# GpSimd's order inside a slot of the expert loop: the split of the expert's activation ahead of the layer chains' step

## The reference, cut to what matters

```python
x = x + 0.5 * moe(layernorm(x))        # 16 experts, top 4, gated: down((up + 1) * glu)
x = x + ssm(layernorm(x))              # long convolution, gelu(exact), projection, inner layernorm
x = x + 0.5 * moe(layernorm(x))        # the same experts again
x = x + 0.5 * lora_moe(layernorm(x))   # 8 + 2 null experts of rank 16, top 2
x = x + attention(layernorm(x))        # 16 heads of 8
x = x + 0.5 * lora_moe(layernorm(x))
```

## The kernel before

| engine | steps |
|---|---|
| VectorE | stats 0, scan_in 5, scan 6, resid 10, inner_stats 11, b_stats 20 |
| GpSimd | norm 0, y 7, gelu_lo 9, inner_norm 12, add 16, b_norm 21 |
| ScalarE | rows 3, gelu 8, inner_rows 14, b_rows 23 |
| TensorE | t1 0, t2 4, proj 10, inner_t1 11, inner_t2 15 |

## Time and profile before

### The profile page before, as it was taken

How to read it: one execution, slowest core, us unless ns; L and a number is a source line. 1 busy time by engine, 2 the same in 40 slices (tenths; PEclk the granted TensorE clock), 3 DMA queues, 4 the chain that set the end, 5 groups by cost and what they waited for, 6 DMA issues and landing times.

```text
span 752.4 us, 11122 instructions
## 1 busy us (share of the span) xinstructions
PE 665.9 (89%) x3617; PEld 389.8 (52%) x3617; DVE 485.5 (65%) x1264; ACT 544.8 (72%) x762; POOL 272.7 (36%) x298
## 2 busy tenths in 40 slices
PE   3798899889999999999876679999999999999857
PEld 2576677667667687777654532322323333333244
DVE  4888979879898999889756542344323445544343
ACT  4765575677768676755334669999999999999722
POOL 3377476866767665556501610112000000000010
PEclk9999999999999999999958789999999999999955
DMA  9001333222332233333200299000099200000000
GB/s 255 29 1 38 111 108 98 86 96 98 90 98 99 88 117 106 99 113 113 64 20 0 66 194 187 4 1 1 15 187 198 51 1 1 2 1 15 16 2 28
DMA packets 31374, 54.54 MB, mean 72 GB/s; under 512 B 4640, under 2 KB 13312, under 8 KB 29808
## 3 DMA queue, kind: packets, MB, share of 16 engines
q1 hardware_dynamic: 30128, 53.38, 26.9%
q0 software_dynamic: 224, 0.34, 0.2%
q10 hardware_dynamic: 960, 0.07, 0.1%
HBM read 35.72 MB, written 1.28 MB: 49 GB/s over the span
## 4 chain that ended last, share of the span: by engine, by line
PE 36%; ACT 23%; DVE 16%; issue 13%; POOL 10%; DMA 1%; ACTq 1%; DVEq 0%; POOLq 0%
ACT raw_w L951 16%; PE bank L1920 7%; POOL act_parts L686 6%; PE bank L1895 5%; PE bank L1596 5%; PE bank L1598 4%; PE bank L1597 4%; DVE act L1215 3%; DVE bank L1204 2%; DVE up L1193 2%; DVE stats L1052 2%; POOL rstd L633 2%; PE bank L1732 1%; ACT xt L777 1%; PE bank L1729 1%
## 5 line engine op out<-in xcount | busy, mean ns | idle before, releaser
L951 ACT ACTIVATE raw_w<-bank,minus_c 128x1024 f32<-128x1024 f32 x256 | 260.8, 1147 | 5.6 <-PE bank L1920 4.5
L686 POOL TENSOR_TENSOR act_parts<-act,act_parts 128x512 fp32r<-128x512 f32 x128 | 168.0, 1316 | 92.8 <-ACT act_parts L850 89.1
L850 ACT ACTIVATE act_parts<-act 128x512 fp32r<-128x512 f32 x128 | 80.8, 632 | 99.9 <-DVE act L1215 99.7
L1440 DVE TENSOR_TENSOR bank<-bank,fix 128x256 f32<-128x256 f32 x128 | 55.3, 433 | 150.8 <-PE bank L1895 150.8
L1596 PE MATMUL bank<-xn_parts,w_hi 128*128 128x512 f32 x256 | 108.3, 423 | 10.2 <-DVE up L1193 6.2
L1193 DVE TENSOR_SCALAR up<-bank,b_up 128x512 f32<-128x512 f32 x128 | 95.3, 744 | 24.4 <-PE bank L1598 21.4
L1598 PE MATMUL bank<-xn_parts,w_hi 128*128 128x512 f32 x256 | 101.4, 396 | 0.0
L1597 PE MATMUL bank<-xn_parts,w_lo 128*128 128x512 f32 x256 | 101.1, 395 | 0.0
L630 POOL TENSOR_SCALAR var_eps<-mean_var 128x4 f32<-128x4 f32 x28 | 6.4, 228 | 231.5 <-DVE mean_var L1056 230.2
L1215 DVE SCALAR_TENSOR_TENSOR act<-up,bank 128x512 f32<-128x512 f32 x128 | 86.6, 676 | 0.0
L836 ACT ACTIVATE bank<-bank,b_gate 128x512 f32<-128x512 f32 x112 | 72.9, 651 | 7.1 <-PE bank L1598 6.8
(11 more groups left out here) (217 smaller groups left out, 1035.1 us busy)
## 6 DMA issues: line engine op xcount, KB each, us to landing
grow<-scores SPq DMA_DIRECT2D x68, 256.0 KB, 3.2
early<-scores SPq DMA_DIRECT2D x44, 256.0 KB, 3.2
raw_w<-in_gate_up SPq DMA_DIRECT2D x4, 512.0 KB, 8.6
w_lo<-gelu_parts SPq DMA_DIRECT2D x8, 256.0 KB, 5.1
w_lo<-act_parts SPq DMA_DIRECT2D x8, 256.0 KB, 5.4
w_hi<-gelu_parts SPq DMA_DIRECT2D x6, 256.0 KB, 4.7
w_hi<-act_parts SPq DMA_DIRECT2D x6, 256.0 KB, 5.6
x_tok<-in_x SPq DMA_DIRECT2D x4, 256.0 KB, 3.9
```

What stands on the lines that cost most here:

```text
L686: pool.tensor_tensor(act_lo[:, j % NACT, :], act[:, j % NACT, :], act_hi[:, j % NACT, :].bitcast(F32), ALU.subtract).then_inc(s["lo_ready" ...
L850: eng.activation(act_hi[:, j % NACT, :], act[:, j % NACT, :], ACT.Copy).then_inc(s["hi_ready"], 1)
L951: eng.activation(probs[:, u % NP, :], pair, ACT.Exp, bias=minus_c[:, b:b + 1])\
```

## The change

In each slot GpSimd makes the low part of job s - 1 first and its chain and single steps after it. No instruction is added or taken away, no semaphore changes its meaning, and the other engines' programs are the same.

```diff
             for slot in range(FIRST_SLOT, JOBS + 1):
-                side("pool", slot, chains, single)
                 if slot >= 1:
                     expert_lo(slot - 1)
+                side("pool", slot, chains, single)
```

## The result

The changed kernel takes 781.39 us (median of 4 runs, 779.59 to 782.69), the kernel before 755.44 us in the 4 runs beside it: a ratio of 1.0347 [1.032, 1.0375], slower. The profiled execution of the changed kernel took 781.63 us, with a span of 779.8 us (752.4 before) and a mean TensorE clock of 0.923 (0.948 before).

What follows compares the result with a forecast made beforehand. VectorE, the engine with least room, was taken to bound the expert loop, delays counting where it goes idle. -4.8 + 17.7 + 3.3 + 1.0 = +17.2, plus 5 for the clock, on 754.17 gave 776.4, stated as 777 us (764 to 788).

Steps and rivals of the forecast that it cites:

- Part 1: Norm steps on GpSimd that hold a low part: turned, TensorE's waits go, -4.8 us, between -3 and -4.8.
- Part 2: `y` and `gelu_lo` behind the low part: gelu and projection late in four chunks, +17.7 us, from +9 to +20.
- Part 3: Eleven norms with statistics a slot earlier now wait for the low part: 0.3 us each, +3.3 us, 0 to 9.
- Part 5: TensorE's clock at the projection stalls: three falls in four, +5 us, from 0 to 14.
- Part 4: Weight splits of slot 8: TensorE waits for the low part of job 8, +1.0 us, from 0 to 1.
- The clock stays up: Rival at the projections: same stalls, no falls of TensorE's clock, 771.4 us; chance 0.20.
- Only `gelu`'s wait: Rival: only gelu's 2.2 us per chunk counts, the low part of job 28 not late, 760 us; chance 0.10.
- The relief wins: Rival: low part already made when `y` gets its scan, so turning costs `y` nothing, 748.5 us; chance 0.05.
- No change: Rival: GpSimd is off the path and both effects are hidden, 754 us; chance 0.04.
- Lasting falls: Rival on TensorE's clock: its falls last, 788 us; chance 0.06.

Runs made afterwards that it cites:

- the added matmuls: Changed kernel plus twelve matmuls with thrown-away results ahead of each projection's wait for `gelu_lo`, to keep TensorE busy: 775.12 us, ratio 1.0274 to the kernel before.

## Why the prediction was right

The forecast was 777 us, from 764 to 788, slower by over 1% with 0.86; measured were 781.39 us and +3.5%. By its parts:

**What bounds the kernel.** That a delay counts where VectorE goes idle for it, and then nearly in full, held: the loss and the gain of each part showed as steps of `up`, and the parts tried alone add up to within some 2 us.

**Part 1**, the first norms: -4.8 us, from -3 to -4.8, was forecast. Alone they give steps of -4.9 (and -0.5 at slot 11) and some -4.0 net. What was given back at the next jobs had not been counted. Right within the range.

**Part 2**, `y` and `gelu_lo`: the mechanism held step by step. `gelu` was forecast 2.2 us late; ScalarE's idle time before it is 2.19. The low part of job 28 was forecast at 116.65 and began at 117.03, the projection at 119.3 and it began at 119.62, in a trace in which `up` was already 0.57 us late ahead of chunk 0. Its stall was forecast at 4.9, 3.8, 4.5 and 4.5 us. The one that could be seen free of the clock, chunk 1's, is 3.8. It has in it the delay by the norm of chunk 0, which the forecast had counted: with `y` and `gelu_lo` alone behind, the step at job 45 is 0.72 and not 1.84. For the others an estimate is left: their steps in the changed kernel (6.5, 6.9, 6.9), each less the 1.8 us that the fall cost in chunk 1, are 4.7, 5.1 and 5.1. The sum is then 18.7 against 17.7. Some 2.1 us of it, at jobs 45, 61 and 77, are also steps of the later norms alone, so Part 3 counts them again; with `y` and `gelu_lo` alone the same estimate gives 23.8 - 7.2 = 16.6.

**Part 5**, the clock, is the term that was too small. No run shows its 5 us for three falls, which was the author's estimate; the runs showed four falls, each at some 1.8 us by chunk 1, an estimate of 7.2 in all. The price of one was nearly right (5 over three is 1.7; 1.8 here, some 1.6 with `y` alone), and the number was wrong. The clock stayed low for some 6.9 to 10.3 us, where it was 3.4 in the earlier trace rows. Two gaps of 2 to 3.5 us follow each other there, one ahead of L1729 and one ahead of the projection, and with either gap alone the falls were 3.4 to 6.7 us. With the added matmuls the clock stood at 1.00 over the 12 us around one of the four stalls, chunk 1's, and at 0.51 to 0.54 behind the others. How long a gap has to be for a fall is not shown: with `y` alone, chunks 2 and 3 had gaps of the same lengths, and only chunk 2 had a fall (0.72 against 1.00 over 12 us).

**Part 3**, the later norms, was forecast at 3.3 us (0 to 9); alone they cost some 4.6 in the loop. The mechanism held, and the mean of 0.3 us each was too low: at job 45 the weighted gate went late by 0.83 us, just past the 0.8 that the forecast took as the most.

**Part 4** had the right size by a wrong mechanism. Its 1.0 us was to be TensorE waiting for the low part of job 8 behind two splits. That matmul ran with no idle time before it:

```profile
57.60 0.40 PE L1732 MATMUL bank<-act_parts,w_hi 128*128 128x512 f32 x1
```

The loss of 1.09 us is at job 7, where VectorE's subtraction takes 1.30 us beside the split of slot 6, and took 0.22 before. In the two pairs of rows above it starts 0.08 and 0.09 us after the split and ends within 0.1 us of it. The prediction didn't think of it, though the split and the subtraction stand in the same slot of the plan.

**Not foreseen at all** were the -1.59 us at job 100, where the clock fall of before is absent, and the +2.4 us behind the loop. Nine of the twelve changed kernels of this study lack that fall, whatever was moved in them, and three still have it (`y` alone, the single steps alone, the changed order with its readers a slot later); what decides it stays open. There is one trace of each kernel, so chance from one execution to the next isn't excluded; over the 19 runs of the kernel before beside the first experiments the mean clock went from 0.947 to 0.957. For the second the mean clock behind the loop was lower (0.70 in 72.1 us against 0.75 in 69.6); no run tells what made it so. That these two nearly cancel, and that Part 4 came out at its size by another mechanism, was luck; what carries the total is parts 2 and 5. Of the first the runs show the chain step by step, of the second the four falls and their price, and not what brings a fall.

**The rivals.** "The clock stays up" is out: four falls. "Only `gelu`'s wait" is what `y` alone does, 766.85 us, and the other half is real. "The relief wins" is out by the point that was named for it: in chunk 0 the high part ended after GpSimd was free, which now shows as 0.91 us of idle GpSimd ahead of the low part at 108.66. The kernel with only the first norms moved gains, but not by way of `y`. "No change" is out by the 3.5%. Lasting falls, which stood at 0.06 and 788 us, are out by the price: the clock was low for longer than the 3.4 us of the earlier trace rows, but a fall cost some 1.8 us.

## What to carry to other kernels

An engine that runs in its written order makes whatever stands behind an item inherit that item's latest input. Before moving an item back, ask when the input of the item now ahead of it arrives, and who waits in order for the moved one. Here the low part's input came 0.9 us after GpSimd was free, and the path through ScalarE's queue led back to GpSimd two jobs on, so one place on GpSimd cost 5.6 to 6.9 us per chunk, the fall of the clock with it. With the readers a slot later the same order cost 3.1 us in the whole loop.

Move items by kind and not the whole list: the same change holds a gain of 0.6% (the norms whose statistics are made in the same slot) and a loss of 3%. And a stall of TensorE is to be priced with the fall of the clock where one comes with it: here 1.8 us on a stall of 3.8, by chunk 1.

## What the runs showed of the hardware that I had not expected

- A VectorE subtraction of 64 columns took 1.30 us beside a GpSimd subtraction that began 0.08 us earlier, and 0.22 in the kernel before, where GpSimd's subtraction of that moment had 0.1 us left.
- The other way round, GpSimd's low part took 2.06 us and not 1.30 beside VectorE's scan (the row at 105.69 above; the scan, L1243, runs from 105.46 to 106.68).
- In chunk 0, with two gaps of 2.0 and 3.3 us on TensorE, the clock fell inside the second and stood at 0.54 over 7.5 us in which matmuls ran for 4.88 us, and in the other chunks at 0.51 to 0.52 over 10.5 us. The fall in the loop of before lasted 3.4 us.
- With `y` alone the longest gap on TensorE at a projection was 1.5 to 2.0 us, and the clock fell to 0.50 in chunks 0, 1 and 2; in chunk 3, with gaps of 1.5, 0.6 and 0.8 us as in chunk 2, it stayed at 1.00 (254 to 266 us).
